# Half-by-half queries at the end of a scan block, norms inside its chunk loop, output products moved, and some matmuls issued twice

## The reference

```python
x = layer0(x, ctx, ctx, mask, ...)   # 16 heads of 16: softmax(QK^T/4, masked) V, Wo, + x, layer norm
h = mamba2(x, ...)                   # in_proj, conv of 4 taps, scan over 512 steps, 8 heads of 64, state 128
                                     # y = (scan + D*xh) * silu(z); u = rms(y)*w; h = x + u @ out_proj_w
xn = ln(h, ca_ln_w, ca_ln_b)         # layer norm
q = xn @ Wq; k = ctx @ Wk; v = ctx @ Wv        # 8 heads of 32
out = h + softmax(q k^T / sqrt(32)) v @ Wo
```

## Time and profile before

| | |
|---|---|
| median of 3 runs | 8527.78 us (8526.52 to 8528.01) |
| profiled execution, own time | 8529.28 us |
| its span in the trace | 8527.6 us |
| PE busy | 7657.0 us (90%) |
| DVE busy | 5273.6 us (62%) |
| ACT busy | 3407.2 us (40%) |
| POOL busy | 1913.5 us (22%) |
| mean granted TensorE clock | 0.933 of 2.4 GHz |

### The profile page before, as it was taken

How to read it: one execution, slowest core, us unless ns; L and a number is a source line. 1 busy time by engine, 2 the same in 40 slices (tenths; PEclk the granted TensorE clock), 3 DMA queues, 4 the chain that set the end, 5 groups by cost and what they waited for, 6 DMA issues and landing times.

```text
span 8527.6 us, 129102 instructions
## 1 busy us (share of the span) xinstructions
PE 7657.0 (90%) x37476; PEld 3496.5 (41%) x37796; DVE 5273.6 (62%) x12605; ACT 3407.2 (40%) x4278; POOL 1913.5 (22%) x1864
## 2 busy tenths in 40 slices
PE   3989999998998989989899899989989899898998
PEld 0353433435334353443534334343343534435343
DVE  3666565765666666666665666656666666666656
ACT  0524435343352434535244352443524345252443
POOL 3040130402203031130401304022030311304113
PEclk6989999899998989999899998999989999998999
DMA  3142230423314132231422304233141332314223
GB/s 73 28 80 38 42 68 10 80 38 51 58 23 75 30 63 55 36 55 28 77 41 37 67 15 80 38 49 60 21 77 31 59 53 34 62 30 73 45 36 63
DMA packets 230684, 422.55 MB, mean 50 GB/s; under 512 B 37209, under 2 KB 128251, under 8 KB 229769
## 3 DMA queue, kind: packets, MB, share of 16 engines
q1 hardware_dynamic: 227927, 413.21, 28.2%
q10 hardware_dynamic: 2048, 0.53, 0.0%
HBM read 191.17 MB, written 8.54 MB: 23 GB/s over the span
## 4 chain that ended last, share of the span: by engine, by line
PE 69%; DVE 12%; issue 8%; ACT 4%; DMA 3%; SPq 2%; POOL 1%; DVEq 1%; ACTq 0%; POOLq 0%
PE ps L1049 12%; PE ps L976 11%; PE ps L938 8%; PE ps L1019 7%; PE ps L1022 6%; DVE mx L1667 5%; PE ps L1024 3%; PE ps L1054 3%; ACT PR L1438 2%; PE ps L1205 2%; PE ps L996 2%; PE ps L1168 2%; PE ps L1259 1%; DVE ps L1702 1%; DMA qst<-qhl 1%
## 5 line engine op out<-in xcount | busy, mean ns | idle before, releaser
L1438 ACT ACTIVATE PR<-ps 128x1024 f32<-128x1024 f32 x2496 | 2503.4, 1024 | 2472.8 <-PE ps L1022 1247.0
L1638 DVE CUSTOM_DVE_ANT_0 ps<-ps,maskq 128x402 f32<-128x402 f32 x4203 | 2410.6, 588 | 1519.8 <-PE ps L976 1372.9
L1049 PE MATMUL ps<-PR,vbuf 128*32 128x512 f32 x9984 | 1343.2, 610 | 29.0 <-ACT PR L1438 24.0
L976 PE MATMUL ps<-kst,qst 96*128 96x402 bf16 (+1 forms) x3115 | 1017.9, 340 | 104.9 <-DVE mx L1638 73.0
L1667 DVE TENSOR_REDUCE mx<-ps 128x2 f32<-128x804 f32 x1024 | 934.1, 988 | 193.8 <-PE ps L996 192.1
L1022 PE MATMUL ps<-maskk,identb 128*128 128x512 bf16 x2592 | 984.9, 380 | 0.0
L1019 PE MATMUL ps<-qst,kst 99*128 99x512 bf16 x2496 | 916.8, 381 | 12.5 <-ACT PR L1438 5.2
L996 PE MATMUL ps<-kst,qst 100*128 100x402 f32 x2048 | 744.1, 489 | 163.6 <-DVE mx L1667 104.8
L1024 PE MATMUL ps<-qst,kst 102*128 102x512 f32 x1664 | 768.0, 526 | 100.3 <-ACT PR L1438 70.9
L976 PEld LDWEIGHTS ps<-kst,qst 96*128 96x128 bf16 x3115 | 281.8, 97 | 1194.4 <-DVE mx L1638 825.5
L756 POOL MEMSET kst<- 96x252 f32 (+1 forms) x34 | 8.7, 256 | 3023.7 <-PE ps L1049 2975.7
(11 more groups left out here) (200 smaller groups left out, 8127.0 us busy)
## 6 DMA issues: line engine op xcount, KB each, us to landing
kst<-khl SPq DMA_DIRECT2D x300, 200.1 KB, 7.5
stage<-in_maskt SPq DMA_DIRECT2D x204, 256.0 KB
stage<-in_mask SPq DMA_DIRECT2D x204, 201.0 KB
kst<-khl SPq DMA_DIRECT2D x96, 402.0 KB, 8.6
kst<-khl SPq DMA_DIRECT2D x96, 398.5 KB, 11.6
ctxs<-in_ctxt SPq DMA_DIRECT2D x17, 1601.0 KB, 17.5
qst<-q1hl SPq DMA_DIRECT2D x96, 256.0 KB
win_s<-in_w_in SPq DMA_DIRECT2D x16, 1288.0 KB, 5.8
```

The costliest lines, as they stand in the source:

```text
L976: pe.matmul(ps[:, bank, 0:w], QS[gi][0:KROWS, h, i * P:(i + 1) * P], KS[gi][0:KROWS, h, c0:c0 + w], start=True, stop=True).then_inc(s_raw, 1)
L1049: mm = pe.matmul(ps[32 * j:32 * j + 32, 6, :], l, PR[:, t % 2, j, :], start=(t == 0), stop=(t == KT - 1), tile_position=(0, 32 * j))
L1438: nc.scalar.activation(PR[:, t % 2, 2 * half:2 * half + 2, :], ps[:, bank:bank + 2, :], ACT.Exp, scale=scale).then_inc(s_p, 1)
L1638: nc.vector.tensor_tensor_reduce(src, src, maskq[:, i, c0:c0 + w], 1.0, -3.0e38, ALU.add, ALU.max, mx[:, c, h * QT + i:h * QT + i + 1]).th ...
```

## The change

Five edits go together.

1. **Norms in the chunk loop.** DVE does `block_out(c - 2)` between two gate steps of chunk `c`, and `rows_out(0)` after the state update of chunk 2. POOL makes one deviation per row block (`deviation1`).
2. **Queries in two halves** of 256 (`HW`) columns, row blocks 0 and 1 and then 2 and 3. Each half has its transposes (`transposes1`, its own bank), its `xn` copies, its query products (`queries1`, banks 5 and 7, then 0 and 1), its split into `q1hl`, and its six stack DMAs (12 where there were 6, each of half the bytes). The first half's transposes stand inside the last `project_block`, between its transposes and its product. `idle` goes from 3 + 3 + 14 matmuls to 2 + 2 + 6. `raw1_place` takes all units of the first query half before those of the second, and a second wait stands ahead of unit 16 of each group.
3. **Partial output products moved up.** In layer 0 the partial products of row block 0 stand ahead of the last `times_v`, those of block 1 behind it, of block 2 ahead of `spread`, of block 3 behind it. In layer 1 `project_out` writes banks 4 to 7 and does block 3 last.
4. **Last 20 raw units twice.** From the 20th entry before the end, `entry1` issues its two matmuls and then the same two again (same operands, same banks). Four `idle` matmuls follow the last entry.
5. **Batch head.** PE's wait for `s_fin` moves from the loop's head to ahead of the first value projection of layer 0, and layer-0 group 0 has its raw entries spread over steps 1 to 12 and no longer over 0 to 12.

The core of the diff:

```diff
-        for n, item in enumerate(LASTQ):
-            pj_bank[item] = n % 2
-               [(FIRST1 + 48, FIRST1 + 110, 0, KT - 1)], [(FIRST1 + 110, FIRST1 + 160, 1, KT - 1)], \
+               [(FIRST1 + 48, FIRST1 + 110, 1, KT - 1)], [(FIRST1 + 110, FIRST1 + 160, 1, KT - 1)], \
         def raw1_place(k):
-            h, i, c = k // (QT * NC // 2), k // (NC // 2) % QT, k % (NC // 2)
+            part, k = k // (UNITS // NHALF), k % (UNITS // NHALF)
+            h, i, c = k // (HT * NC // 2), part * HT + k // (NC // 2) % HT, k % (NC // 2)
-        XT1_BANK = [2, 4]
+        XT1_BANK = [4, 2]
+        Q1_BANK = [[5, 7], [0, 1]]
+        NHALF = 2
+        IDLE = 6
+        TWICE = 20
...
-                for g in range(G1):
-                    stack_q1(b, g)
+                for part in range(NHALF):
+                    for g in range(G1):
+                        stack_q1(b, part, g)
...
+                deviation1(0)
+                scale_u(QT - 2)
+                deviation1(1)
+                scale_u(QT - 1)
+                deviation1(2)
+                deviation1(3)
...
+                if kind == "raw" and k == UNITS // NHALF:
+                    pe.wait_ge(s_qs1[g][1], LEAD + (b + 1) * STACKQ1[1])
...
-                for e in range(2):
+                for e in (0, 1) * (2 if n >= NENT1 - TWICE else 1):
                     mm = pe.matmul(ps[:, bank + e, 0:CW], QS1[g][0:MROW1 + 1, h, i * P:(i + 1) * P],
...
+                    if gi == 0 and t == 0:
+                        pe.wait_ge(s_fin, LEAD + b * QT)
+                    if gi == G0 - 1 and t == KT:
+                        pe.wait_ge(s_norm, LEAD + b * NG + G0 - 1)
+                        pe.wait_ge(s_p, (b * NG + G0) * KT * 2 - 1)
+                        project_out(wo0_s, 0, G0 - 1, G0, range(1))
                     if t >= 1:
                         times_v(b, gi, t - 1, between)
...
-                pe.wait_ge(s_fin, LEAD + b * QT)
...
+                project_out(wo0_s, 0, G0 - 1, G0, range(1, 2))
                 sums(b, G0 - 1)
...
-                project_out(wo0_s, 0, G0 - 1, G0, range(1))
+                project_out(wo0_s, 0, G0 - 1, G0, range(2, 3))
                 spread(b, G0 - 1)
-                project_out(wo0_s, 0, G0 - 1, G0, range(1, QT))
+                project_out(wo0_s, 0, G0 - 1, G0, range(3, QT))
...
+                def transposes1(part):
+
+                    for i in range(part * HT, (part + 1) * HT):
+                        pe.wait_ge(s_xs1, b * QT + i + 1)
+                        for k in range(DT):
+                            col = k * HW + (i - part * HT) * P
+                            mm = pe.transpose(ps[:, XT1_BANK[part], col:col + P], xs1[:, i, k * P:(k + 1) * P], ident[:, :])
+                    mm.then_inc(s_xst1, 1)
+
+                def queries1(part):
+
+                    pe.wait_ge(s_xn1, (NHALF * b + part + 1) * DT)
+                    for n, item in enumerate(LASTQ):
+                        for k in range(DT):
+                            mm = pe.matmul(ps[:, Q1_BANK[part][n], 0:HW], wq1_s[:, k, n * P:(n + 1) * P],
+                                           xn[:, k, part * HW:(part + 1) * HW], start=(k == 0), stop=(k == DT - 1))
+                        mm.then_inc(s_qp1, 1)
+
+                pe.wait_ge(s_ti, (b + 1) * (QT - 1))
+                pe.wait_ge(s_h, LEAD + (b + 1) * (QT - 1))
+                project_block(QT - 1, lambda: transposes1(0))
+                queries1(0)
                 pe.wait_ge(s_tj, (b + 1) * (QT - 1))
-                idle(3, 1)
...
+                idle(2, 1)
+                transposes1(1)
+                idle(2, 1)
+                queries1(1)
+                idle(IDLE, 6)
...
-                pe.wait_ge(s_q1, (b + 1) * DT)
+                pe.wait_ge(s_q1, (b + 1) * DT * NHALF)
...
                 pe.wait_ge(s_rest, rests(b + 1, FRONT[-1]) + 1)
+                idle(4, 7)
                 pe.wait_ge(s_r1free, LEAD + (b + 1) * NENT1)
...
+                for e in LAST1:
+                    left(b + 1, e)
+                project_out(wo1_s, 0, G1 - 1, G1, range(1), 4)
                 spread(b, NG - 1)
-                project_out(wo1_s, 0, G1 - 1, G1, range(1, QT))
+                pe.wait_ge(s_ctxn, LEAD + b * NG + NG)
+                project_out(wo1_s, 0, G1 - 1, G1, range(1, QT - 1), 4)
                 pe.wait_ge(s_norm, LEAD + b * NG + NG)
-                project_out(wo1_s, G1 - 1, G1, G1)
+                project_out(wo1_s, G1 - 1, G1, G1, range(QT - 1), 4)
+                project_out(wo1_s, 0, G1, G1, range(QT - 1, QT), 4)
```

More of the change, by code:

```diff
@@ L1082, in spread, with project_out @@
                 mm.then_inc(s_spread, 1)
+            def project_out(wo, lo, hi, n, tiles=range(QT), first=0):
+                for i in tiles:
+                    for g in range(lo, hi):
+                        mm = pe.matmul(ps[:, first + i, 0:D], ctxn[:, g, i * P:(i + 1) * P], wo[:, g, :],
+                                       start=(g == 0), stop=(g == n - 1))
+                    if hi == n:
+                        mm.then_inc(s_o, 1)
             def group(b, gi):
@@ L1250, in project_block @@
                     mm.then_inc(s_gt, 1)
+                    if beside_copy is not None:
+                        beside_copy()
                     pe.wait_ge(s_ut, b * QT + c + 1)
```

157 lines of the change are left out of this document (69 added, 88 removed).

## The result

| | before | after |
|---|---|---|
| median, us | 8527.15 (4 runs, 8522.94 to 8528.01) | 8244.52 (4 runs, 8230.98 to 8273.27) |
| ratio | | 0.967 [0.965, 0.970] |
| profiled execution: time, span | 8529.3, see above | 8254.75, 8252.8 |
| mean granted clock | 0.933 | 0.968 |

The change takes 283 us away where 264 were forecast; 8244.5 lies in the range of 8220 to 8335, on the fast side. Now they lie 42 us apart, which the forecast did not foresee; the experiments show where in a batch the spread lies.

A forecast was written before the change was run, and what follows sets the result against it. PE, on the chain for 69%, bounds the kernel through its waits and half-clock work. Terms of 9.4 + 0.7 + 2.3 + 3.7 = 16.1 us, times 16, plus 15 x 0.4, gave 263.6 off 8529.3: forecast 8265 us, range 8220 to 8335.

The forecast's parts named there:

- 312 us after the loop's head: Sign of being right: the first raw matmul stands some 312 us after the loop's head, where it was 321.4.
- Term 1: Tail of layer 0 up to the first raw unit: raw work begins 9.4 us sooner per batch, bounds 6 to 11.
- Term 2: Raw stage of layer 1: 0.7 us gained per batch, from a faster first projection less costs of doubled units and POOL.
- The even chance that the first projection meets the full clock: Raw stage: the first forward projection may meet full clock, gaining between 0 and 2.0 us, taken as 1.0.
- Term 3: Start of layer-1 attention: full clock at the first score gains 2.3 us per batch, bounds 0 and 3.7.
- Term 4: End of layer 0: moved output products bring DVE's first layer-norm addition 3.7 us sooner per batch, bounds 1.8 and 3.9.
- Term 5: Batch boundary: PE's moved wait and 12 packed steps gain 0.4 us, 15 times, between -1 and 1.5.
- The clock did not fall in the tail: Rival judged: in the tail PE drops to 1.2 GHz, giving back some 6 of 9.4 us, 8362 us; 8%.
- Half-width copies did not pay per row: Rival judged: 1 KB rows of stack copies take as long as 2 KB ones, 13 us given back, 8474 us; 4%.
- the third: Rival in the raw stage: doubled units meet half clock for some 5 units, 3.8 us, 8326 us; 8%.
- the slower case: Rival: PE never regains full clock in the raw stage's last 20 units, 17.5 us lost, 8546 or more; 3%.
- More than summed: Rival: the raw stage loses all stalls and the tail starts at 4167, 19.5 us gained, 8215 us; 9%.

The follow-up runs named there:

- the fastest kernel: The changed kernel with the old batch head and three of the seven raw units ahead of each projection doubled, besides the last 20: 8209.3 us, ratio 0.962.

## Why the prediction was right, and where it was not

The sum is nearer than its terms, and part of that is luck: terms 1 to 3 gave 3.6 us per batch more than forecast, terms 4 and 5 gave 2.3 less, and 0.4 was lost between the layer norm and the scan, which no term names. The sign "312 us after the loop's head" did not follow from the forecast's own terms: it takes off the 9.4 of the tail but not the 3.7 of term 4 and the 0.4 of term 5, which makes 308; measured in the mean are 308.5, where 321.6 were.

**Term 1, the tail.** Right in mechanism, mis-sized: 9.4 forecast, 11.6 measured. The chain that was walked came out 0.5 shorter than summed (8.87 for 9.4), which makes 10.0 of gain; in the mean the batches gave 1.35 more ahead of it, between the first dx and the last `rows_out`. That piece is the clock: before the change every batch but the first had a half-clock stretch of 6.8 us in the first chunks (49.7 to 42.9 us ahead of its first raw matmul), after it only the long ones have it. With this stretch the last `block_out` starts 33.61 us after the first `dx` in both kernels, without it 30.73 in the changed one; the forecast's "`block_out(3)` begins at 4159.01 as before" is right, and its 9.4 left out what the clock gives. Of the parts, whole stacks cost 157 us and norms behind the loop 87; that `block_out` fits into DVE's wait for PE held (0.79 us of it are left of 1.93 in chunk 3). The queries in halves with their moved transposes were not taken back by themselves.

**Term 2, the raw stage.** 1.4 for 0.7. The even chance that the first projection meets the full clock is what tells the batches apart: it does in 11 of 15, and in the long kind it does not. The 0.3 put down for the doubled units was not found: the reductions take 985 ns with them and 984 without, and the shortest raw stages are 59.4 us in both kernels. The Trainium skill ("TensorE: Matmul & The Clock Gate", Part 1, the section on a second failure mode) says of one kernel that short idle gaps between groups of matmuls make the clock swing. The raw stage with single units agrees: before the change it has four stretches at half clock, from 1.5, 18.6, 32.3 and 45.9 us after its start. In the batch shown of the kernel without doubling PE pauses some 0.26 us per unit until the clock falls at 43 us, and in the batch shown of the change it stays whole there with doubled units.

**Term 3, the start of layer 1.** The size was near, 3.0 for 2.3; the idle matmuls account for 2.7 of it, and the other 0.3, up to the next head, is open, since the end of layer 1 has a new order too that no run takes back. The step that failed is "the doubled units are 0.83 us of matmul in every 0.905, and the four idle matmuls fill the wait", which gave the full clock to both: without the idle matmuls it is lost whether or not units are doubled (6.80 us), without doubling it is kept (5.08). It is lost with the pause of 1.87 us right ahead of the first score.

**Term 4, the end of layer 0.** 3.16 for 3.7; taken back, it costs 2.5 directly. In the kernel before, this phase took from 8.47 to 10.11 us. The forecast walked from a batch of 10.11, where the gain is 3.5, and counted it for all; in 3 of the 15 whole batches the phase took 8.5 us, not 10.1.

**Term 5, the boundary.** The step "packed into 12 steps, which costs some of it" was mis-sized so far that the sign turned: forecast a gain of 0.4, measured 1.36 later than before, of which the experiment with the old head shows 1.14. One step without raw entries saves 1.7 us once, and 0.26 us in the mean of 11 distances costs 2.8, half of it in the one where PE waits for DVE's row maxima.

**The rivals.** The clock did not fall in the tail. Two windows of the batch shown above, both with transposes in them (the first has four at 2021.85, the second those of block 3):

```profile
2020.00:2024.00 4.00, 3.75 (x22) 3.15 (x21) 1.33 (x4) 2.18 (x5) 1.47 (x4) 1.00 0.00 0
2024.00:2028.00 4.00, 3.68 (x20) 3.00 (x19) 2.62 (x7) 0.95 (x2) 1.54 (x5) 1.00 0.00 0
```

No batch of the changed kernel has half clock there. By the rule quoted from the Trainium skill it would have fallen; in the kernel with norms behind the loop it does fall, with transposes that have pauses around them, and no run tells which of the two does it. Half-width copies did not pay per row. While they ran the queue moved more than the 120 GB/s it moved with whole ones:

```profile
2034.00:2036.00 2.00, 1.65 (x8) 1.03 (x6) 1.63 (x2) 0.00 (x0) 0.00 (x0) 1.00 1.17 140
```

In this batch a packet of these copies, of 1 KB, takes 116 ns in the mean; in the batch of the earlier trace rows one of 2 KB takes 258. The doubled units met no half clock in any batch, and the reductions there are 0.90 us apart, so neither the third nor the slower case came. "More than summed" was nearest to the truth in direction, with 283 us against 264, but its mechanism did not come: the raw stage keeps part of its stalls.

**What was not foreseen** is that the stretches at half clock move about, and some come or go, with every edit. Total time at half clock fell from 1152 to 526 us, 434 in the fastest kernel; it does not rank the kernels, for with nothing doubled it is 718 and the time no longer. The same scan and raw instructions cost 34.5 + 61.1 us in the changed kernel and 36.05 + 62.6 with layer 0's products moved back, which stand some 70 us ahead of the scan and 110 ahead of the raw stage. This is what makes single edits worth up to twice their direct price and more (99 for 41), and it tells the batches of one execution apart. That the 42 us between runs have the same cause is argued from that, for each trace is of one execution. That a mere shift of a batch in time is enough for this is argued from the stretches' places, not shown by itself: no kernel moved a batch by a known time and changed nothing else. Also open is how much the doubled units gain where they stand in the change; taking them away gave 8 us less time, inside the interval.

## What to carry to other kernels

Walk the chain behind the stage you change link by link from its rows, as for the tail here, where it came out within a tenth; but when PE's clock switches many times in a batch, ask of every edit also which pauses it leaves in front of dense work, since they move stretches elsewhere. A pause of PE of about 2 us right ahead of a stage that depends on its speed was worth filling with matmuls that nobody reads (2.7 us per batch here); doubling work where another engine sets the pace was worth nothing for itself here, and 0.5 us through the matmuls right behind it. Work taken out of one loop step and packed into the others is costed by each step that gets longer, not by the one that got shorter; look first for the step in which another engine was already late.

## What the runs showed of the hardware

- A single pause of 1.87 us, after 18 us of dense matmuls at full clock, was followed by some 10 us at 1.2 GHz; with four matmuls that nobody reads in that pause, the phase behind it is at full clock in every batch of the change (4.93 to 5.20 us for 6.80).
- Six matmuls that nobody reads, ahead of the raw stage, start it 0.8 us later and make it 2.5 us shorter in the mean; net it is 1.2 us per batch by the medians, whose intervals just overlap.
- The same program shows batches from 498 to 507 us side by side in one execution, told apart by where the half-clock stretches lie; with more raw units doubled and the old batch head, all batches but the outer two lie within 1.3 us of each other.
- Two matmuls of 402 columns per 0.9 us kept up with the reductions at either clock: 984 ns, and in the windows at 0.50 DVE is busy 4.00 of 4.00 us, as at 1.00.
- Copies between tiles in SBUF moved 140 GB/s with rows of 1 KB and 120 with rows of 2 KB; a packet took 116 and 258 ns.
